# Delta recurrence: products that share an operand joined (48 in place of 80 a step), in two chains half a step apart, with keys and queries interleaved by chunk

## The chip, the cores and the metric

The kernel runs on one core of one Trainium2 chip. The metric is the device time of one execution in microseconds (us). A run gives one time; the figure quoted for a kernel is the median of its runs.

## The reference, cut to what matters

Four model layers follow one another over `x`, 16 sequences of 512 tokens with 128 channels. The change lies in the mixing part of layer 1, a gated delta rule with 4 heads of 32 channels, in chunks of 32 tokens (16 chunks a sequence):

```python
def _delta_rule(q, k, v, beta):
    ...
    v = v * beta[..., None]
    kb = k * beta[..., None]
    ...
    A = jnp.where(tril_strict, kb @ jnp.swapaxes(k, -1, -2), 0.0)
    inv = solve_triangular(eye + A, jnp.broadcast_to(eye, A.shape), lower=True)
    u = inv @ v
    w = inv @ kb
    ...
    def step(S, xs):
        q_i, k_i, u_i, w_i = xs
        attn = jnp.where(tril, q_i @ jnp.swapaxes(k_i, -1, -2), 0.0)
        u_adj = u_i - w_i @ S
        o_i = q_i @ S + attn @ u_adj
        S = S + jnp.swapaxes(k_i, -1, -2) @ u_adj
        return (S, o_i)
    S, o = jax.lax.scan(step, S0, (qs, ks, us, ws))
```

Both kernels compute `u_adj` as `inv @ (v - kb @ S)`, so that `inv` is applied once. The state `S` of a head is 32x32 and runs through the 16 chunks one after the other; 16 sequences by 4 heads are independent.

## The kernel before, in words

The program is written engine by engine: each engine (PE, DVE, ACT, POOL, and SP for the DMAs) has its own list of instructions in a fixed order, and semaphores tie them together. There is no scheduler; the order written is the order run. `l1_attn` (L1085 on) runs five phases with a barrier of all engines between them: `delta_inputs`, `delta_inverse`, `delta_recurrence`, `long_convolutions`, `delta_output`. The first three hand their tensors on through DRAM (`k.d`, one 128x512 array a sequence and name).

`delta_inputs` (L1104 on) handles one sequence a round: projections, filters, norms, and at the end on DVE `scale` (L1183 on) and `mask_products` (L1199 on), which write the tensors that the recurrence reads: `k` (tokens of a chunk by channels), `qT` and `kbT` (channels by tokens), `vb`, `a` and `attnT`. Every one is 128x512: row block h (32 rows) is head h, column block n (32 columns) is chunk n. SP stores 8 tensors a round (L1306). `delta_inverse` makes `inverseT` from `a`.

`delta_recurrence` (L1393 on) takes 4 sequences (G) at a time, a group; 4 groups run after one another, the first unrolled, the other three in a hardware loop (`over_groups`). A group has 16 steps, one a chunk. In a step all 4 sequences by 4 heads go through the same products, 16 products of 32x32 by 32x32 each, on the diagonal tiles of the array (rows and columns of head h): `tiles`, L1454. In the order of PE (`run` in the PE block):

- `ps_r` = kb S; DVE (L1512) makes `r` = vb - ps_r;
- `ps_u` = inv r; ACT (L1546) copies it to `u`;
- `ps_s` = kᵀ u; DVE (L1516) adds it to the state, which goes back and forth between two buffers;
- `ps_o` = q S + attn u of the step before, 32 products, in two halves put into the places where PE waits for `r` and for `u`; ACT (L1538) copies it out.

That is 80 products a step. In the loop a small `carrier` product (L1461) stands ahead of each wait. Every 4 steps, a quarter, DVE transposes the quarter's output (L1526), SP stores it and loads the same quarter of the next group: 6 loads of 128 partitions by 4 sequences by 128 columns (L1428), one store (L1434). All four quarters of a group are loaded before the first starts.

## Time and profile before

| what | value |
|---|---|
| median of 3 runs | 5998.68 us (5989.8 to 6001.67) |
| the profiled execution: its time | 5983.12 us |
| the profiled execution: its span | 5981.3 us |
| busy over the span: PE / weight loads / DVE / ACT / POOL | 75% / 47% / 67% / 39% / 30% |
| mean granted TensorE clock | 0.833 of full speed |

The span is the time from the first to the last instruction of the profiled execution. Busy shares are means over twelve stages with different limits; the change touches two phases of one stage. Rows name lines of the kernel before (L1454), engines (PE matmul, PEld weight load, DVE VectorE, ACT ScalarE, SPq the DMA issues of SyncE) and tiles by the program's names without buffer numbers; most tiles of the recurrence lie in a spare tensor and so are shown as `convolved`. "issue" as the reason of a wait means that the engine waited for nothing that the profile shows. An f32 matmul is shown as two weight loads and two matmuls, so 16 products are 32 matmul rows.

### The profile page before, as it was taken

Reading aid. Unit: us, or ns where it says so; the run is one execution under the profiler, and the core shown is the slowest. Engines: PE = TensorE matmul, PEld = TensorE weight load, DVE = VectorE, ACT = ScalarE, POOL = GpSimd, SP = SyncE. Lnnn points to the kernel's source line nnn. Section 1 sums busy time; section 2 is a strip of 40 time slices with the busy share of each in tenths; the row PEclk is TensorE's granted clock in tenths of the full one; section 3 lists DMA queues with packets and bytes.
Section 4 is the critical chain, followed back from the end, with each engine's and each line's share of the span. In section 5 each row is a group of like instructions: output and inputs, shape, how many; then the busy total and the mean of one; then the engine's idle time right before and its main releaser. Section 6 shows DMA issues by size and latency. Waiting matters only on the chain. (4 is left out here: it accounts for less than half of the span.)

```text
span 5981.3 us, 117856 instructions
## 1 busy us (share of the span) xinstructions
PE 4490.3 (75%) x44057; PEld 2811.6 (47%) x44057; DVE 4032.7 (67%) x9213; ACT 2353.0 (39%) x4425; POOL 1785.9 (30%) x2265
## 2 busy tenths in 40 slices
PE   4699998596720665674966669999666799888998
PEld 3122222484410554453744434544344577666776
DVE  6688885787977112786879757777698455485553
ACT  3488887202410103442111146666311344323443
POOL 2455552212433000233124334443244111163110
PEclk9699999798865557765987769999877899888999
DMA  1222220001331425100000023222000000000001
GB/s 41 50 51 51 51 51 19 6 1 49 117 94 38 114 77 104 52 32 21 1 1 0 3 51 63 58 53 52 1 0 0 20 0 0 1 1 1 0 0 29
DMA packets 229468, 203.06 MB, mean 34 GB/s; under 512 B 24067, under 2 KB 202879, under 8 KB 228399
## 3 DMA queue, kind: packets, MB, share of 16 engines
q1 hardware_dynamic: 229039, 197.19, 14.2%
q8 instruction: 288, 4.72, 0.3%
q14 instruction: 141, 1.16, 0.1%
HBM read 118.89 MB, written 72.88 MB: 32 GB/s over the span
## 5 line engine op out<-in xcount | busy, mean ns | idle before, releaser
L534 DVE TENSOR_REDUCE rotary_maxima<-rotary_ps_s 128x1 f32<-128x512 f32 x1024 | 644.3, 684 | 120.1 <-PE rotary_ps_s L697 118.2
L534 DVE TENSOR_REDUCE alibi_maxima<-alibi_ps_s 128x1 f32<-128x128 f32 (+3 forms) x1024 | 451.8, 485 | 233.0 <-PE alibi_ps_s L705 226.3
L782 ACT ACTIVATE rotary_probs<-rotary_ps_s 128x512 f32<-128x512 f32 x1024 | 552.5, 596 | 130.6 <-PE rotary_ps_s L721 128.1
L2161 DVE SCALAR_TENSOR_TENSOR x<-moe_ps_out,moe_weights,x 128x128 f32 (+1 forms) x1024 | 285.6, 344 | 458.2 <-PE moe_ps_out L2202 430.5
L2202 PEld LDWEIGHTS moe_ps_out<-w_moe_w,moe_hidden 128*128 128x128 f32 x4096 | 495.0, 192 | 108.2 <-issue 80.4
L2202 PE MATMUL moe_ps_out<-w_moe_w,moe_hidden 128*128 128x128 f32 x4096 | 500.6, 275 | 0.0
L2189 PE MATMUL moe_ps_hidden<-moe_z,w_moe_w 128*128 128x512 f32 x1024 | 488.7, 600 | 0.0
L2251 ACT ACTIVATE moe_hidden<-moe_ps_hidden,w_moe_b 128x512 f32<-128x512 f32 x512 | 345.6, 687 | 360.2 <-PE moe_ps_hidden L2189 348.4
L782 ACT ACTIVATE alibi_probs<-alibi_ps_s 128x512 f32<-128x512 f32 (+3 forms) x1024 | 394.4, 440 | 214.4 <-PE alibi_ps_s L729 211.3
L697 PE MATMUL rotary_ps_s<-rotary_k_stack,rotary_q_stack 64*128 64x512 bf16 x1024 | 251.2, 404 | 49.6 <-DMA rotary_k_stack<-rotary_parts 25.0
L217 POOL TENSOR_TENSOR moe_rstd<-moe_meanvar,eps 128x4 f32<-128x4 f32 x64 | 12.8, 201 | 907.7 <-DVE moe_meanvar L190 907.7
L662 PE MATMUL rotary_ps_pv<-rotary_probs,rotary_v 128*32 128x512 f32 x2048 | 277.4, 614 | 2.8 <-ACT rotary_probs L782 1.2
L1025 PE MATMUL moe_ps_out<-w_moe_w,moe_weighed 128*128 128x128 f32 x2048 | 270.2, 287 | 1.9 <-DVE moe_weighed L960 1.9
L1025 PEld LDWEIGHTS moe_ps_out<-w_moe_w,moe_weighed 128*128 128x128 f32 x2048 | 246.7, 197 | 39.2 <-issue 33.1
L2054 PE MATMUL fp_ps_gate<-w_fp_gate,fp_normedT 128*128 128x352 f32 x256 | 141.3, 643 | 149.7 <-DVE fp_hidden L2015 127.7
L697 PE MATMUL alibi_ps_s<-alibi_k_stack,alibi_q_stack 64*128 64x128 bf16 (+3 forms) x1024 | 209.0, 316 | 54.1 <-DMA alibi_k_stack<-alibi_parts 28.4
L697 PEld LDWEIGHTS rotary_ps_s<-rotary_k_stack,rotary_q_stack 64*128 64x128 bf16 x1024 | 64.7, 93 | 385.9 <-DVE rotary_maxima L534 291.8
L721 PE MATMUL rotary_ps_s<-rotary_q_stack,rotary_k_stack 64*128 64x512 bf16 x1024 | 220.8, 382 | 21.3 <-ACT rotary_probs L782 12.5
L2189 PEld LDWEIGHTS moe_ps_hidden<-moe_z,w_moe_w 128*128 128x128 f32 x1024 | 175.7, 192 | 128.2 <-issue 123.9
L1454 PE MATMUL delta_state_ps_r<-convolved 32*32 32x32 f32 x2048 | 44.6, 239 | 251.5 <-DMA convolved<-delta_attnT 237.3
L1546 ACT COPY convolved<-delta_state_ps_u 128x128 f32<-128x128 f32 x64 | 17.0, 266 | 493.6 <-PE delta_state_ps_u L1454 493.6
L960 DVE TENSOR_TENSOR moe_weighed<-moe_normedT,moe_ps_spread 128x1024 f32<-128x1024 f32 x128 | 152.6, 1211 | 81.9 <-PE moe_ps_spread L1016 81.9
(488 smaller groups left out, 10715.2 us busy)
## 6 DMA issues: line engine op xcount, KB each, us to landing
rotary_parts<-rotary_part SPq DMA_DIRECT2D x96, 128.0 KB, 2.2
rotary_q_stack<-rotary_parts SPq DMA_DIRECT2D x192, 64.0 KB
rotary_k_stack<-rotary_parts SPq DMA_DIRECT2D x192, 64.0 KB
convolve_bands<-in_filters SPq DMA_DIRECT2D x192, 64.0 KB, 2.6
alibi_parts<-alibi_part SPq DMA_DIRECT2D x96, 128.0 KB, 2.4
alibi_q_stack<-alibi_parts SPq DMA_DIRECT2D x192, 64.0 KB
alibi_k_stack<-alibi_parts SPq DMA_DIRECT2D x192, 64.0 KB
delta_n<-convolved SPq DMA_DIRECT2D x16, 256.0 KB, 2.0
```

The costliest lines, as they stand in the source:

```text
L534: v.tensor_reduce(maxima[:, blk, 2 * pair + two:2 * pair + two + 1], ps_s1[(j - 1 + u) % 3][:, 0:keys_of(blk)], AXIS.X, ALU.max).then_inc( ...
L662: last = mm(ps_pv[32 * g:32 * g + 32, lo:T], va[jv][:, kb, 4 * qd + g, :], probs[4 * (group % 2) + g][:, 0:T - lo], start=(kb == 0), stop= ...
L697: last = mm(ps_s1[(jb + u) % 3][:, 0:n], qs[jb][rows, pair, blk * P:(blk + 1) * P], ks[jb][rows, pair, 0:n], start=True, stop=not causal)
L721: last = mm(ps_s2[(jc + u) % 3][:, 0:T - lo], ks[jc][rows, pair, kb * P:(kb + 1) * P], qs[jc][rows, pair, lo:T], start=True, stop=not causal)
L782: nc.scalar.activation(probs[u % 8][:, 0:T - lo], ps_s2[(j - 2 + u) % 3][:, 0:T - lo], ACT.Exp).then_inc(s.exp_made, 1)
L960: v.tensor_tensor(weighed[n][:], nT, ps_spread[n % 2][:], ALU.mult).then_inc(s.inputs_weighed, 1)
L1025: last = mm(ps_out[i % 2][:, b, :], weighed[n][:, m, b * P:(b + 1) * P], w.moe1_w[:, 2 * n + m, :], start=(n + m + b == 0), stop=False)
L2054: nc.tensor.matmul(ps_gate[b % 2][:], nT[:, b * P:(b + 1) * P], w.fp4_gate[:, 0:F], start=True, stop=True).then_inc(s.gate_done, 1)
L2161: v.scalar_tensor_tensor(xb, ps_out[e % 2][:, b:b + 1, :], weights[par][:, b, e:e + 1], xb, ALU.mult, ALU.add).then_inc(s.added, 1)
L2189: mm(ps_hidden[(2 * e + h) % RING][:], w.moe3_w1[:, e, h * P:(h + 1) * P], z[par][:], start=True, stop=True).then_inc(s.hidden_done, 1)
L2202: last = mm(ps_out[e % 2][:, b, :], hidden[e % 2][:, h, b * P:(b + 1) * P], w.moe3_w2[:, e, h, :], start=(h == 0), stop=(h == 1))
L2251: nc.scalar.activation(hidden[e % 2][:, h, :], ps_hidden[(2 * e + h) % RING][:], ACT.Gelu, bias=w.moe3_b1[:, e, h:h + 1]).then_inc(s.hidde ...
```

## The change

`delta_inputs` writes two wide tensors in place of four: `kq`, in which for each chunk the 32 columns of `kbT` and the 32 of `qT` stand side by side, and `ku`, the same for `k` and `attnT`. SP stores 6 tensors a round. The arithmetic is the same; DVE writes `k`, `attnT`, `qT` and `kbT` with a stride of 64 columns a chunk.

`delta_recurrence` has three blocks of 16 products a step: `first` (`kq` against the state: kb S and q S at once, 64 output rows), `make_u` (inv r), `third` (`ku` against u: the step of the state and attn u at once, 64 output rows). The operands of `first` and of `make_u` lie on the partitions 0 to 31 (heads 0 and 1) and 64 to 95 (heads 2 and 3); heads 0 and 1 differ by a column offset. `make_r`, the sum of the state and the new sum of the output (`o1` + attn u) on DVE, and the copy `keep_o1` on ACT, go over 128x256. Two chains of 4 sequences run half a step apart; two turns of 16 double steps handle the 16 sequences; nothing is in a hardware loop. Each chain has two buffers a quarter of input: 13 loads a quarter and chain (12 of 32 partitions, one of 128), 4 stores.

```diff
-                 for n in ("a", "inverseT", "kbT", "qT", "k", "vb", "attnT", "n", "v", "o")}
+                 for n in ("a", "inverseT", "kq", "ku", "vb", "n", "v", "o")}
...
+    kq, ku = [[ph.sb(f"{n}{j}", [P, CHUNKS, 2, CHUNK]) for j in range(2)] for n in ("kq", "ku")]
...
-                k_out, qT_out, kbT_out = [out[n][par] for n in ("k", "qT", "kbT")]
+                k_out, qT_out, kbT_out = ku[par][:, :, 0, :], kq[par][:, :, 1, :], kq[par][:, :, 0, :]
...
-                v.transpose(qT_out[:], qn[:]).then_inc(s.back_turned, 1)
+                v.transpose(qT_out, by_chunk(qn)).then_inc(s.back_turned, 1)
...
+    rows = lambda h: slice(h * DH, (h + 1) * DH)
+    low = lambda h: slice(h // 2 * 2 * DH, (h // 2 * 2 + 1) * DH)
+    pair = lambda h: slice(h // 2 * 2 * DH, (h // 2 + 1) * 2 * DH)
...
+            def load(g, c, q):
+                j = q % RING
+                for h in range(GH):
+                    for to, name in ((kq, "kq"), (vb, "vb"), (inverseT, "inverseT")):
+                        sp.dma_start(flat(to[c][j][low(h), h % 2]), seq_rows(name, g, c, q)[rows(h)]).then_inc(loaded[c][j], 16)
+                sp.dma_start(flat(ku[c][j][:]), seq_rows("ku", g, c, q)).then_inc(loaded[c][j], 16)
...
+                        sp.wait_ge(o_turned[c], Q * g + q + 1)
+                        if q + RING < Q:
+                            load(g, c, q + RING)
+                        elif g + 1 < turns:
+                            load(g + 1, c, q + RING - Q)
+                        for h in range(GH):
+                            sp.dma_start(seq_rows("o", g, c, q)[rows(h)], o_cm[c][q % RING][h // 2 * 2 * DH + DH:h // 2 * 2 * DH + 2 * DH, h % 2]).then_inc(stored[c][q % RING], 16)
...
+            def first(g, c, i):
...
+                pe.wait_ge(state_made[c], n + g + 1)
+                at_least(pe, o1_kept[c], n)
+                for b in range(G):
+                    for h in range(GH):
+                        last = mm(ps_first[c][pair(h), h % 2, b, :], kq[c][q % RING][low(h), h % 2, b, i % Q, :],
+                                  state[c][i % 2][low(h), h % 2, b, :], start=True, stop=True)
...
+            def make_u(g, c, i):
...
+                        last = mm(ps_u[c][rows(h), b, :], inverseT[c][q % RING][low(h), h % 2, b, i % Q, :], r[c][low(h), h % 2, b, :],
+                                  start=True, stop=True)
...
+            def third(g, c, i):
...
+                        last = mm(ps_third[c][pair(h), h % 2, b * DH:(b + 1) * DH], ku[c][q % RING][rows(h), b, i % Q, :],
+                                  u[c][rows(h), b, :], start=True, stop=True)
...
                 for i in range(CHUNKS):
+                    first(g, 0, i)
+                    if i:
+                        third(g, 1, i - 1)
+                    make_u(g, 0, i)
+                    first(g, 1, i)
+                    third(g, 0, i)
+                    make_u(g, 1, i)
+                third(g, 1, CHUNKS - 1)
...
+                v.tensor_tensor(r[c][:], vb[c][q % RING][:, :, :, i % Q, :], ps_first[c][:], ALU.subtract).then_inc(r_made[c], 1)
...
+                v.tensor_tensor(state[c][(i + 1) % 2][:], state[c][i % 2][:], thirds[c], ALU.add).then_inc(state_made[c], 1)
...
+                v.tensor_tensor(o_hc[c][i // Q % 2][:, :, :, i % Q, :], o1[c][:], thirds[c], ALU.add).then_inc(o_added[c], 1)
...
                 for i in range(CHUNKS):
+                    make_r(g, 0, i)
+                    if i:
+                        add(g, 1, i - 1)
                     if i and i % Q == 0:
+                        turn(g, 1, i // Q - 1)
+                    make_r(g, 1, i)
+                    add(g, 0, i)
+                    if i % Q == Q - 1:
+                        turn(g, 0, i // Q)
...
+                    keep_o1(g, 0, i)
+                    keep_u(g, 0, i)
+                    keep_o1(g, 1, i)
+                    keep_u(g, 1, i)
```

On PE, in the recurrence, one step of the kernel before (the second of a group: r, half of o, u, the other half of o, s, and the next r) reads:

```order
L1454 MATMUL delta_state_ps_r<-convolved 32x32 x16
L1454 MATMUL delta_state_ps_o0<-convolved 32x32 x16
L1454 MATMUL delta_state_ps_u<-convolved 32x32 x16
L1454 MATMUL delta_state_ps_o0<-convolved 32x32 x16
L1454 MATMUL delta_state_ps_s<-convolved 32x32 x16
```

In the changed kernel one double step, a step of each chain (the number after `first`, `u` and `third` is the chain), reads on PE:

```order
L1475 MATMUL delta_state_ps_first0<-convolved 64x32 x16
L1495 MATMUL delta_state_ps_third1<-convolved 64x32 x16
L1484 MATMUL delta_state_ps_u0<-convolved 32x32 x16
L1475 MATMUL delta_state_ps_first1<-convolved 64x32 x16
L1495 MATMUL delta_state_ps_third0<-convolved 64x32 x16
L1484 MATMUL delta_state_ps_u1<-convolved 32x32 x16
```

A step of 5 blocks of 16 has become 3 blocks of 16, and behind each block of one chain stands a block of the other; `third1` belongs to the step before.

On SP, one load of a quarter for 4 sequences in the kernel before, six issues:

```order
L1428 DMA convolved<-delta_kbT 128x4x128
L1428 DMA convolved<-delta_vb 128x4x128
L1428 DMA convolved<-delta_inverseT 128x4x128
L1428 DMA convolved<-delta_k 128x4x128
L1428 DMA convolved<-delta_qT 128x4x128
L1428 DMA convolved<-delta_attnT 128x4x128
```

In the changed kernel the same quarter of one chain begins with the three rows of head 0, which follow three times more for heads 1 to 3, and ends with `ku`; the stores of an earlier quarter come behind it:

```order
L1442 DMA convolved<-delta_kq 32x4x256
L1442 DMA convolved<-delta_vb 32x4x128
L1442 DMA convolved<-delta_inverseT 32x4x128
...
L1443 DMA convolved<-delta_ku 128x4x256
L1456 DMA delta_o<-delta_state_o_cm00 32x4x128 x4
```

Six loads and a store have become 13 loads and 4 stores, with the same bytes; the store, which stood ahead of the loads, stands behind them.

## Rows read from the trace of the kernel before

**Rows 1.** Busy time by stretch: `delta_inputs`, then the recurrence's lead-in, steps, end.
```profile
core 0: us, PE busy (x) PEld busy (x) DVE busy (x) ACT busy (x) POOL busy (x), PEclk, DMA share, GB/s
1385.00:1725.00 340.00, 206.99 (x4533) 121.40 (x4531) 275.92 (x583) 130.11 (x192) 115.75 (x64) 0.80 0.29 105
1937.00:1944.50 7.50, 0.00 (x0) 0.00 (x0) 0.17 (x1) 0.00 (x0) 0.00 (x0) 0.50 0.82 229
1944.50:2271.20 326.70, 221.21 (x10432) 186.60 (x10432) 48.71 (x147) 34.09 (x128) 0.00 (x0) 0.50 0.33 88
2271.20:2275.70 4.50, 0.00 (x0) 0.00 (x0) 0.00 (x0) 0.00 (x0) 0.00 (x0) 0.50 0.19 58
```

**Rows 2.** Waits of PE, 1944 to 2275: us in total, times, longest us.
```profile
PE delta_state_ps_o L1454 <- issue: 32.2, 34, 3.1
...
PE delta_state_ps_s L1454 <- issue: 14.8, 14, 1.3
PE delta_state_ps_u L1454 <- issue: 11.4, 13, 2.3
PE delta_state_ps_r L1454 <- issue: 7.8, 11, 1.5
PE delta_state_ps_carrier L1461 <- issue: 7.2, 2, 3.7
```

**Rows 3.** DMA queues, 1945 to 2271: packets, MB, share of 16 engines.
```profile
q1 hardware_dynamic: 54870, 27.24, 30.6%
q8 instruction: 84, 1.38, 1.8%
```

**Rows 4.** Timeline of PE, 2127 to 2136: start, us, instruction, [idle before <- releaser].
```profile
2127.50 0.65 PE L1454 MATMUL delta_state_ps_r<-convolved 32*32 32x32 f32 x31 [0.15 <-issue]
...
2129.33 0.63 PE L1454 MATMUL delta_state_ps_o<-convolved 32*32 32x32 f32 x30
2131.39 0.26 PE L1454 MATMUL delta_state_ps_o<-convolved 32*32 32x32 f32 x2 [1.43 <-issue]
...
2135.39 0.28 PE L1454 MATMUL delta_state_ps_u<-convolved 32*32 32x32 f32 x4 [0.55 <-issue]
```

**Rows 5.** DMA queues, 1950 to 2024, the first group, with the loads of the second.
```profile
q1 hardware_dynamic: 17099, 8.49, 43.0%
q8 instruction: 19, 0.31, 1.7%
```

**Rows 6.** DMA queues, 2189 to 2271, the last group, which loads nothing further.
```profile
q1 hardware_dynamic: 5280, 2.62, 11.6%
q8 instruction: 23, 0.38, 1.8%
```

**Rows 7.** Groups by line and shape, 1944.5 to 2271.2: busy us, mean ns, idle before.
```profile
L1454 PE MATMUL delta_state_ps_r<-convolved 32*32 32x32 f32 x2048 | 44.6, 239 | 251.5 <-DMA convolved<-delta_attnT 237.3 <-issue 7.8 <-DVE convolved L1516 6.4
...
L1516 DVE TENSOR_TENSOR convolved<-convolved,delta_state_ps_s 128x128 f32<-128x128 f32 x64 | 18.4, 288 | 208.0 <-PE delta_state_ps_s L1454 208.0
L1512 DVE TENSOR_TENSOR convolved<-convolved,delta_state_ps_r 128x128 f32<-128x128 f32 x64 | 18.4, 288 | 70.1 <-PE delta_state_ps_r L1454 68.7
...
L1546 ACT COPY convolved<-delta_state_ps_u 128x128 f32<-128x128 f32 x64 | 17.0, 266 | 493.6 <-PE delta_state_ps_u L1454 493.6
L1526 DVE STREAM_TRANSPOSE convolved<-convolved 128x512 f32<-128x512 f32 x16 | 11.4, 711 | 6.8 <-ACT convolved L1538 6.3
```

**Rows 8.** Groups by line and shape, whole run: a wider DVE operation and one transpose.
```profile
L862 DVE TENSOR_TENSOR moe_more<-moe_more,moe_same 128x256 f32<-128x256 f32 x32 | 13.6, 425 | 1.1
...
L1193 DVE STREAM_TRANSPOSE convolved<-convolved 128x512 f32<-128x512 f32 x16 | 11.3, 705 | 0.0
```

**Rows 9.** Timeline of SP, 1936 to 2140: DMA issues, the first loads and later ones.
```profile
1937.26 0.40 SPq L1428 DMA_DIRECT2D convolved<-delta_kbT  x1
1937.71 0.50 SPq L1428 DMA_DIRECT2D convolved<-delta_vb  x1
...
1939.91 0.71 SPq L1428 DMA_DIRECT2D convolved<-delta_attnT  x1
...
1945.75 0.83 SPq L1428 DMA_DIRECT2D convolved<-delta_kbT  x1
```

**Rows 10.** Timeline of PE, 2340 to 2343, `long_convolutions`: 64-column tiles over all rows.
```profile
2340.32 0.94 PE L1614 MATMUL convolve_ps_y<-convolve_windows,convolve_bands 128*64 128x64 f32 x24 [0.80 <-DMA convolve_bands<-in_filters]
```

**Rows 11.** Busy time by stretch: loads of `a` in `delta_inverse`, 16 partitions each, 8 apart.
```profile
1726.00:1740.00 14.00, 0.00 (x0) 0.00 (x0) 0.97 (x1) 0.00 (x0) 9.00 (x1) 0.50 1.13 193
```

More of the change, by code:

```diff
@@ L1407, in delta_recurrence @@
-    state = [ph.sb(f"state{j}", [P, G, DH]) for j in range(2)]
-    o_hc = [ph.sb(f"o_hc{j}", [P, G, Q, DH]) for j in range(2)]
-    o_cm = [ph.sb(f"o_cm{j}", [P, G, Q * DH]) for j in range(Q)]
-    ps_r, ps_u, ps_s = ph.ps("r", [P, G, DH]), ph.ps("u", [P, G, DH]), ph.ps("s", [P, G, DH])
-    ps_o = [ph.ps(f"o{j}", [P, G, DH]) for j in range(2)]
-    ps_carrier = ph.ps("carrier", [DH, 1])
-    groups = seqs // G
-    seq_rows = lambda name, g, q: d[name][bass.ds(g * G, G), :, q * (T // Q):(q + 1) * (T // Q)].rearrange("s p t -> p s t")
@@ L1416, in over_groups @@
-    def over_groups(eng, run):
-        run(0)
-        if groups > 1:
-            with eng.Fori(1, groups) as g:
-                run(g)
+    CHAINS = 2
+    RING = 2
+    LOADS = 3 * GH + 1
+    per_chain = "first_done r_made o1_kept u_done u_made third_done state_made o_added o_turned".split()
+    s = [ph.signals(" ".join([f"{n}{c}" for n in per_chain] + [f"loaded{c}_{j} stored{c}_{j}" for j in range(RING)])) for c in range(CHAINS)]
+    first_done, r_made, o1_kept, u_done, u_made, third_done, state_made, o_added, o_turned = [
+        [s[c][n] for c in range(CHAINS)] for n in range(len(per_chain))]
@@ new lines, in delta_recurrence @@
+    r, o1 = [[ph.sb(f"{n}{c}", [P, 2, G, DH]) for c in range(CHAINS)] for n in ("r", "o1")]
+    u = [ph.sb(f"u{c}", [P, G, DH]) for c in range(CHAINS)]
+    state = [[ph.sb(f"state{c}{j}", [P, 2, G, DH]) for j in range(2)] for c in range(CHAINS)]
+    o_hc = [[ph.sb(f"o_hc{c}{j}", [P, 2, G, Q, DH]) for j in range(2)] for c in range(CHAINS)]
+    o_cm = [[ph.sb(f"o_cm{c}{j}", [P, 2, G, Q * DH]) for j in range(RING)] for c in range(CHAINS)]
+    ps_first = [ph.ps(f"first{c}", [P, 2, G, DH]) for c in range(CHAINS)]
@@ new lines, in delta_recurrence, with seq_rows @@
+    ps_u = [ph.ps(f"u{c}", [P, G, DH]) for c in range(CHAINS)]
+    ps_third = [ph.ps(f"third{c}", [P, 2, T]) for c in range(CHAINS)]
+    thirds = [ps_third[c][:, :, 0:G * DH].rearrange("p e (b v) -> p e b v", v=DH) for c in range(CHAINS)]
+    turns = seqs // (G * CHAINS)
+    rows = lambda h: slice(h * DH, (h + 1) * DH)
+    low = lambda h: slice(h // 2 * 2 * DH, (h // 2 * 2 + 1) * DH)
+    pair = lambda h: slice(h // 2 * 2 * DH, (h // 2 + 1) * 2 * DH)
+    def seq_rows(name, g, c, q):
+        wide = d[name].shape[2] // Q
+        first = (CHAINS * g + c) * G
+        return d[name][first:first + G, :, q * wide:(q + 1) * wide].rearrange("s p t -> p s t")
@@ L1422, in delta_recurrence @@
+    flat = lambda t: t.rearrange("p b n e -> p b (n e)")
     with nc.Block() as block:
@@ L1448, in _ @@
             mm = nc.tensor.matmul
-            def tiles(to, left, right, start=True, stop=True, sequences=range(G)):
-                for b in sequences:
-                    for h in range(GH):
-                        at = slice(h * DH, h * DH + DH)
-                        last = mm(to[at, b, :], left[at, b, :], right[at, b, :], start=start, stop=stop)
-                return last
-            def ready(sem, value):
-                at_least(pe, sem, value)
-                if not isinstance(value, int):
-                    mm(ps_carrier[0:DH, 0:1], k.ident16[:, 0:DH], k.ident16[:, 0:1], start=True, stop=True)
@@ L1463, in results @@
-            def results(g, i, sequences):
-                if 0 in sequences:
-                    ready(s.o_read, CHUNKS * g + i - 1)
-                q, c = i // Q, slice((i % Q) * CHUNK, (i % Q + 1) * CHUNK)
-                for b in sequences:
-                    tiles(ps_o[i % 2], t["qT"][:, q, :, c], state[i % 2], stop=False, sequences=[b])
-                    last = tiles(ps_o[i % 2], t["attnT"][:, q, :, c], u[i % 2], start=False, sequences=[b])
-                if G - 1 in sequences:
-                    last.then_inc(s.o_done, 1)
@@ L1522, in turn, with make_r @@
-            def turn(g, q):
-                dve.wait_ge(s.o_read, CHUNKS * g + Q * q + Q)
-                at_least(dve, stored[q], 16 * g)
-                v.transpose(o_cm[q][:].rearrange("p b t -> p (b t)"),
-                            o_hc[q % 2][:].rearrange("p b n e -> p (b n e)")).then_inc(s.o_turned, 1)
-            over_groups(dve, run)
+            def make_r(g, c, i):
+                n, q = CHUNKS * g + i, i // Q
+                dve.wait_ge(first_done[c], n + 1)
+                if i % Q == 0:
+                    dve.wait_ge(loaded[c][q % RING], here(g, q))
+                at_least(dve, u_done[c], n)
+                v.tensor_tensor(r[c][:], vb[c][q % RING][:, :, :, i % Q, :], ps_first[c][:], ALU.subtract).then_inc(r_made[c], 1)
```

164 lines of the change are left out of this document (77 added, 87 removed).

## The prediction

> **What bounds the kernel now.** I began with the busy time by stretch [rows 1]. The recurrence has three stretches: a lead-in of 7.5 us with no product, 326.7 us of steps, and an end of 4.5 us, together 338.7 us. In the steps DVE is busy for 48.7 us and ACT for 34.1 us, PE for 221 us, and the DMA engines for a third. No engine is full, so the waits come next. Among PE's waits [rows 2] five rows name "issue": 32.2 + 14.8 + 11.4 + 7.8 + 7.2 = 73.4 us in 74 pieces. PE then waited for nothing that a semaphore shows. The DMA queues [rows 3] show 84 packets of instructions, 1.38 MB, so 16.4 KB each, in this stretch; PE has 2 x 10432 loads and matmuls in it, 248 a packet. The timeline [rows 4] shows a stall at 2127.50, one of 1.43 us before 2131.39 and one of 0.55 us before 2135.39: 3.9 and 4.0 us apart, with 31 + 1 + 32 + 1 + 32 + 30 = 127 matmuls between the first two (of which some rows are left out), thus 254 records. So PE stops at each packet's end until the next has come, about 0.87 us each time (73.4 / 84). A packet every 3.89 us (326.7 / 84) is what PE lives on. With 43% of the DMA engines taken, 19 packets came in 74 us, 3.89 us each [rows 5]; with 11.6% taken, 23 in 82 us, 3.57 us each [rows 6]. This is the reader's main point: time goes with the **number of PE instructions**. The granted clock is 0.50 throughout [rows 1], the 1.2 GHz level; a rise would change nothing in a sum paced by packets.
>
> The other part of a step is the chain through the engines: r on DVE 288 ns, the state on DVE 288 ns, u on ACT 266 ns, three blocks of matmuls [rows 7], each 0.65 us for 16 products [rows 4].
>
> **The change, part by part.**
>
> *Fewer products.* Before there are 64 steps of 4 sequences with 80 products each, 5120 (with 192 carriers 10432 matmuls, two a product). Now there are 32 double steps of 2 x 4 sequences with 96 products each, 3072: 6144 matmuls, 12288 records, and at 248 a packet 49.5 packets.
>
> *What a double step takes without stalls.* One chain's round: `first` takes 0.82 + 0.24 us, as heads 0 and 1 use the same tiles of the array and I let its products start at half the pace of the 0.65 us block (0.41 us for its starts, 0.24 for the last one); make_r 0.425 us, for 128x256 on DVE [rows 8]; make_u 0.65; keep_u 0.27; third 0.65; the state 0.425. Sum 3.48 us. The other chain's block often stands ahead on PE, whose starts alone take 2 x (0.82 + 0.41 + 0.41) = 3.28 us. DVE has 6 x 0.425 and half a transpose of 1024 columns (2 x 0.705 [rows 8], each chain every fourth step: 0.7 us a double step), 3.25 us. I take 4.5 us, between 3.48 (perfect overlap) and twice that, 6.96 (none).
>
> *What the packets make of it.* A double step has 384 records, 1.55 packets. At 4.0 us a packet that is 6.2 us, above 4.5, so **the instructions' supply covers the longer DVE operations, `keep_o1`, the second chain's order on PE and the lost carriers**; if that cover is gone, 4.5 us are left (rival A). Read the other way, as 0.87 us of stall added to the work, it is 4.5 + 1.55 x 0.87 = 5.85 us, nearly the same. I take 4.0 us a packet rather than 3.89, since the same bytes come in less time: 27.24 MB [rows 3] at 30.6% of 326.7 us are 50% of 200 us, more than the 43% of the first group. 49.5 x 4.0 = **198 us**. Ends: 3.57 us, the quiet group, gives 177; 4.5 us, twice as far above the quiet group as the loaded one is and a little more, 223.
>
> *Lead-in.* Before, six issues and 3.6 us to the last landing. Now the first chain waits for 13 issues. Those early ones come 0.45 to 0.53 us apart (1937.26, 1937.71, the sixth at 1939.91) [rows 9]: 6.5 + 3.6 = **10 us**, instead of 7.5. Ends: 9 and 17 us (13 x 0.85, the later spacing, + 3.6 + some 2 for the other chain's).
>
> *End.* 4.5 us now; three more stores at 0.4 us, half a transpose more 0.7, and eight more semaphores to clear, for which no row stands: between nothing and an issue's 0.4 us each I take 0.6 us in all, nearer to nothing, as all 18 of before lie within the 4.5 us. That makes **7 us**, between 6 and 10.
>
> *SP's queue.* Seventeen issues for each chain and quarter, 16 of these. Later issues take 0.83 us [rows 9], so 14.5 us for one group and 231 us in all at that spacing; at 0.45 us 122. They run beside the steps, 4 double steps of 6.2 us = 25 us for two such groups. At 0.45 us (15 us) they are hidden, at 0.83 us (29 us) they aren't: rival C. Nothing else waits on SP; a load stands behind the wait for `o_turned`, the stores behind the loads, so `o_cm` comes free later by 11 issues, which a ring of two quarters covers.
>
> *`delta_inputs`.* DVE is its bound, 276 of 340 us [rows 1]. Six stores rather than eight then cost and give nothing. The strided writes: the nearest rows are `make_r` before, which reads `vb` with a stride between blocks of 32 columns, and the state's add, which does not: both 288 ns [rows 7]. Hence I take 0. Upper end: three transposes of 0.705 us doubled in 16 rounds, 34 us; lower end 0, as no operation is shortened.
>
> *Sum.* 198 + 10 + 7 = 215 us for 338.7, a gain of 123 us. The profiled execution took 5983.1 us, 15.6 below the median of the three runs, 5998.7; 5998.7 - 123 = **5876 us**. By the ends of the packets (177 and 223) 5855 and 5901, with the other terms' ends about 5850 to 5910.
>
> **The rivals.**
>
> *A, the supply isn't what binds.* If the stalls come from something that the changed order doesn't meet, a double step takes 4.5 us: 32 x 4.5 + 17 = 161, a gain of 178, 5821 us. Against it: 74 stalls in 84 packets, in every group [rows 2, 3]. The Trainium skill (Runtime: NRT & Kernel Launch, "Instruction fetch mechanics") says that the engine's memory is refilled in blocks of 16 KiB, 256 instructions, while the current one runs, and that this is hidden by the rate of issue. The size agrees with the 16.4 KB and 248 of these rows; that it is hidden does not. Chance 0.10.
>
> *B, the shared rows make PE slow.* Heads 0 and 1 of `first` and `make_u` load their weights from the same 32 rows. If each such load waits for the matmul ahead of it, `first` starts a matmul every 60 ns, not 26, and make_u every 30: I take the 30 from the 24 matmuls of the convolution, which all share their rows, (0.94 - 0.24) / 23 us [rows 10], and double it for two heads on one tile. PE then has 2 x (1.92 + 0.97 + 0.41) = 6.6 us a double step, 8.0 with stalls; at the middle, 7.3, 234 + 17 = 251 us, a gain of 88: 5911 us. Rows 10 alone, at 30 ns for both, would stay under the packets' 6.2 us, which speaks against B. The Trainium skill (TensorE: Matmul & The Clock Gate, "Part 3: Packing small matmuls") speaks for B: a weight load overlaps a running matmul only where the row group differs, and the change brings four row groups down to two. Chance 0.10.
>
> *C, SP's queue binds.* At 0.83 us an issue the 16 groups take 231 us; with the lead-in and end 248, a gain of 91, 5908 us. For it: the spacing while the first loads are in flight [rows 9]; against it: the average of DMA activity, which stays near half. Chance 0.12.
>
> *E, the chains don't overlap.* Then 6.96 us and 1.35 of stalls, 32 x 8.3 + 17 = 283 us: 5943 us. Against it: the order on PE puts a block of the other chain behind each block. Chance 0.05.
>
> *D, slower.* 12 of 13 loads, and all stores, touch 32 neighbouring partitions. If such a transfer gets a quarter of the rate, 229 GB/s in the lead-in of before [rows 1], thus 57, then a chain's quarter (1.05 MB so, 0.52 MB in `ku`, 0.26 MB out) takes 18.3 + 2.3 + 4.6 = 25 us, and 16 of them 403 us: with 17 us 82 more than before, 6081 us. It decides from (338.7 - 17) / 16 = 20 us a group on. Against it: loads of 16 partitions ran at 193 GB/s [rows 11]; but their partitions lie 8 apart, so this doesn't exclude D. Chance 0.08.
>
> **How the numbers follow.** 0.2% is 12 us, about what a measurement of this kernel can tell from no change. The forecast has 0.55, with 5850 to 5910 as its own range; A 0.10, B 0.10, C 0.12, E 0.05, all faster by far more than 12 us: 0.92. D's 0.08 reaches from break-even up; I give 0.01 of it to no change and 0.07 to slower. The range 5820 to 5925 holds the forecast, B, C and the upper half of A; left out are D, E, the rest of A, and a tail of the forecast, 0.2.
>
> **What would show it.** Right: about 50 packets of instructions between the first and the last product, stalls by "issue" every 127 matmuls or so, double steps near 6.2 us, and the stage near 215 us; DVE at 425 ns, the clock at 0.50; `delta_inputs` still 340 us with the same transposes. C shows as PE's waits for `loaded` ahead of a quarter; B as a `first` far above 1.06 us; A as steps of 4.5 us without stalls; D as loads that land after more than 15 us. Wrong would be the forecast if PE waits mostly for DVE or ACT, for then the chain and not the supply sets the pace.

## The result, and the profile after

The changed kernel takes 5890.6 us (median of 4 runs, 5886.28 to 5895.65), the kernel before on the same chip 5994.24 us. The ratio is 0.9832, 95% interval 0.9819 to 0.9844. The forecast was 5876 us with a range of 5820 to 5925: sign and range held. The gain is 103.6 us where 123 were forecast. The profile shows that the number came out near for another reason than the one given.

The profiled execution took 5886.28 us. First the busy time by stretch: `delta_inputs`, then the recurrence's lead-in to the first product, the time from there to the second chain's first product, the steps, and the end.

```profile
core 0: us, PE busy (x) PEld busy (x) DVE busy (x) ACT busy (x) POOL busy (x), PEclk, DMA share, GB/s
1385.00:1725.00 340.00, 208.66 (x4538) 122.39 (x4537) 275.05 (x584) 129.92 (x192) 115.65 (x64) 0.80 0.28 105
1938.57:1947.93 9.36, 0.00 (x0) 0.00 (x0) 0.54 (x2) 0.00 (x0) 0.00 (x0) 0.50 0.69 193
1947.93:1955.01 7.08, 2.58 (x64) 2.32 (x64) 0.42 (x1) 0.64 (x2) 0.00 (x0) 0.50 1.14 239
1955.01:2169.80 214.79, 211.01 (x6072) 201.01 (x6076) 92.72 (x206) 40.14 (x126) 0.00 (x0) 0.50 0.45 122
2169.80:2178.35 8.55, 0.44 (x18) 0.30 (x12) 2.49 (x4) 0.00 (x0) 0.00 (x0) 0.50 0.26 62
```

The recurrence takes 9.36 + 7.08 + 214.79 + 8.55 = 239.8 us in place of 338.7. In the steps PE is busy for 211.0 of 214.8 us; before, it was busy for 221 of 327 [rows 1]. The waits of PE in the recurrence say the same (238.6 us of the first row are the phase ahead of it, in which PE has nothing to do; the other 4.0 are the second chain's wait for its loads):

```profile
PE delta_state_ps_first L1475 <- DMA convolved<-delta_ku: 242.6, 2, 238.6
PE delta_state_ps_first L1475 <- issue: 2.5, 1, 2.5
PE delta_state_ps_u L1484 <- DVE convolved L1519: 1.0, 2, 0.5
PE delta_state_ps_third L1495 <- ACT convolved L1568: 0.8, 2, 0.4
```

"issue" has gone from 73.4 us in 74 pieces [rows 2] to one piece of 2.5 us, and the waits for DVE and ACT are 1.8 us in all. The packets of instructions come as before; the DMA queues from 1955 to 2170:

```profile
q8 instruction: 48, 0.79, 1.6%
```

48 packets in 215 us are one in 4.48 us, slower than the 3.57 to 3.89 us of the kernel before [rows 5, 6]. So in the changed kernel it is PE that takes its time with a packet, and the next one is there when it is wanted. What PE does with the time is in its timeline, two half steps:

```profile
1957.73 0.65 PE L1484 MATMUL delta_state_ps_u<-convolved 32*32 32x32 f32 x32
1958.34 1.80 PE L1475 MATMUL delta_state_ps_first<-convolved 32*64 32x32 f32 x29
...
1959.98 1.14 PE L1495 MATMUL delta_state_ps_third<-convolved 32*64 32x32 f32 x30
1961.06 0.65 PE L1484 MATMUL delta_state_ps_u<-convolved 32*32 32x32 f32 x32
1961.66 1.80 PE L1475 MATMUL delta_state_ps_first<-convolved 32*64 32x32 f32 x29
```

A half step is 3.33 us (1957.73 to 1961.06), a double step 6.65, without a gap: 0.61 us until `first` starts, 1.64 until most of `third` starts, 1.08 until the next `u`. `first` has 29 of its matmuls in 1.80 us; less 0.29 us for the last one that is 1.51 / 28 = 54 ns from start to start. `third`, with the same shape, has (1.14 - 0.29) / 29 = 29 ns, `u` (0.65 - 0.24) / 31 = 13 ns. The groups by line and shape:

```profile
L1475 PE MATMUL delta_state_ps_first<-convolved 32*64 32x32 f32 x2048 | 123.9, 291 | 245.1 <-DMA convolved<-delta_ku 242.6 <-issue 2.5
...
L1495 PE MATMUL delta_state_ps_third<-convolved 32*64 32x32 f32 x2048 | 81.2, 290 | 0.8 <-ACT convolved L1568 0.8
...
L1484 PE MATMUL delta_state_ps_u<-convolved 32*32 32x32 f32 x2048 | 41.7, 239 | 1.0 <-DVE convolved L1519 1.0
...
L1519 DVE TENSOR_TENSOR convolved<-convolved,delta_state_ps_first 128x256 f32<-128x256 f32 x64 | 27.0, 422 | 109.1 <-PE delta_state_ps_first L1475 109.1
```

`first` alone holds PE for 123.9 us, more than half of the steps. Its heads 0 and 1 load weights of 64 columns into the same 32 rows and 64 columns of the array. `third` has the same weights' width, but its heads lie on rows of their own; `u` shares rows, but each head has columns of its own. Call the rows and columns of the array that a product uses its tile: `first` then works on two tiles, `third` and `u` on four.

### The profile page after: what moved, and what is told of

Same layout as the page of the kernel before. It is cut to its first block and busy times, and to the rows that moved or that the text cites. A ratio compares the mean times of both kernels' runs of the same rounds, so it can differ in the third digit from the quotient of the medians.

```text
span 5884.5 us, 109248 instructions
## 1 busy us (share of the span) xinstructions
PE 4476.3 (76%) x39769; PEld 2821.3 (48%) x39769; DVE 4080.4 (69%) x9277; ACT 2358.3 (40%) x4425; POOL 1782.7 (30%) x2265
## 5 line engine op out<-in xcount | busy, mean ns | idle before, releaser
L1475 PE MATMUL delta_state_ps_first<-convolved 32*64 32x32 f32 x2048 | 123.9, 291 | 245.1 <-DMA convolved<-delta_ku 242.6
L1475 PEld LDWEIGHTS delta_state_ps_first<-convolved 32*64 32x64 f32 x2048 | 115.7, 215 | 251.0 <-DMA convolved<-delta_ku 242.8
```

The costliest lines, as they stand in the source:

```text
L1475: last = mm(ps_first[c][pair(h), h % 2, b, :], kq[c][q % RING][low(h), h % 2, b, i % Q, :], state[c][i % 2][low(h), h % 2, b, :], start=Tr ...
```

## The experiments

The theory after the result has two parts. **Tiles**: `first` is slow because its products go to only two tiles of 32 rows by 64 columns, one for two heads, where they follow one another; that weight load and matmul take turns there, as the expectations below have it, is an assumption that no run tests. **Supply**: packets of instructions come at a limited pace, and bind where PE would be faster than that, as before the change. Rivals are the order of the heads in PE's queue, shared rows as such, a cost added at each packet's end, and the chain through DVE and ACT. In the table the recurrence runs from its first load to the first load of the next phase (338.5 before, by this measure); `delta_inputs` from its first to its last instruction; "issue" is the sum of PE's stalls by issue in the recurrence.

| kernel | time, us | recurrence | `delta_inputs` | issue |
|---|---|---|---|---|
| before | 5994.24 | 338.5 | 314.3 | 73.4 |
| changed | 5890.6 | 239.8 | 315.2 | 2.5 |
| heads_order | 5875.09 (one run) | 242.9 | 310.7 | 3.3 |
| split_first | 5912.87 (one run) | 287.1 | 313.6 | 74.8 |
| rows4 | 5906.23 | 225.3 | 342.5 | 33.9 |
| apart | 5949.43 (one run) | 304.0 | 313.9 | 2.5 |
| rows4b | 5871.52 | 231.6 | 319.2 | 38.3 |
| no_o | 5901.9 (one run) | 257.3 | 313.7 | 17.4 |
| no_loads | 5868.16 (one run) | 209.5 | 319.7 | 16.0 |
| rows4c | 5868.38 | 218.4 | 320.6 | 23.5 |
| changed_again | 5893.39 | 242.3 | 309.5 | 3.5 |
| rows4c_again | 5868.83 | 217.0 | 319.0 | 23.9 |

Single times differ by some 15 us with nothing changed in the stage (heads_order against the changed kernel), and the kernels ran on several chips, so the stage is what the single runs are read by.

**heads_order.**

```diff
-                    for h in range(GH):
+                    for h in (0, 2, 1, 3):
                         last = mm(ps_first[c][pair(h), h % 2, b, :], kq[c][q % RING][low(h), h % 2, b, i % Q, :],
```

> The heads of `first` are taken in the order 0, 2, 1, 3, all else as changed. Theory 1 (tiles): heads 0 and 1 share one tile of 32 rows by 64 columns, heads 2 and 3 another, and on a tile weight load and matmul take turns, 107 ns a matmul; both tiles already run side by side, so the order does not matter: `first` stays at 1.7 us for its starts, a half step at 3.33 us, the recurrence at 240 us (within 3). Rival (order): PE takes its queue in order and a product behind one on the same tile holds up the rest; alternating tiles then lets `first` fall to the pace of `third`, 33 ns a matmul, 1.07 us: 64 x 0.64 = 41 us less, 199 us.

Measured: no gain, 242.9 us, as the changed kernel itself had in a later run (242.3, below). The timeline of its PE has the same spacing, 3.33 us from `u` to `u`:

```profile
2053.82 0.65 PE L1484 MATMUL delta_state_ps_u<-convolved 32*32 32x32 f32 x32
2054.45 1.80 PE L1475 MATMUL delta_state_ps_first<-convolved 32*64 32x32 f32 x29
...
2057.15 0.65 PE L1484 MATMUL delta_state_ps_u<-convolved 32*32 32x32 f32 x32
```

The order of the heads does not matter; the rival falls.

**split_first.**

```diff
-                    for h in range(GH):
-                        last = mm(ps_first[c][pair(h), h % 2, b, :], kq[c][q % RING][low(h), h % 2, b, i % Q, :],
+                    for a in range(2):
+                        for h in range(GH):
+                            last = mm(ps_first[c][rows(h // 2 * 2 + a), h % 2, b, :], kq[c][q % RING][low(h), h % 2, b, i % Q, a * CHUNK:(a + 1) * CHUNK],
```

> `first` is split again into two products of 32 columns a head, kb S and q S, on the same 32 rows but on column tiles of their own (128 products a double step in place of 96). Theory 1 (tiles) alone: such products run like make_u, 19 ns a matmul, so `first` takes 64 x 0.019 = 1.2 us in place of 1.7 and a half step 2.9 us in place of 3.33: 27 us less than 240. Theory 2 (instruction supply, the forecast's): 512 records a double step are 2.06 packets at 3.57 to 4.0 us, 7.4 to 8.3 us in place of 6.65: 23 to 52 us more, with PE's stalls by issue back. If weight loads on shared rows never overlap (the skill's rule, rival B), `first` gets no shorter and the double step is at least 6.65 us.

Measured: 287.1 us, 47 more, inside the supply's 23 to 52. Its PE timeline and the waits:

```profile
2052.07 0.65 PE L1485 MATMUL delta_state_ps_u<-convolved 32*32 32x32 f32 x32
2052.65 1.15 PE L1476 MATMUL delta_state_ps_first<-convolved 32*32 32x32 f32 x64
2053.74 1.06 PE L1496 MATMUL delta_state_ps_third<-convolved 32*64 32x32 f32 x29
2055.76 0.42 PE L1496 MATMUL delta_state_ps_third<-convolved 32*64 32x32 f32 x3 [0.97 <-issue]
```

```profile
PE delta_state_ps_u L1485 <- issue: 35.0, 25, 3.9
PE delta_state_ps_third L1496 <- issue: 33.4, 31, 3.0
PE delta_state_ps_first L1476 <- issue: 6.4, 6, 2.5
```

Both parts show at once. The same arithmetic in twice as many products of half the width takes 1.15 us in place of 1.8: (1.15 - 0.24) / 63 = 14 ns a matmul. Heads 0 and 1 are on the same 32 rows as before, and they still share each tile; but kb S and q S now have columns of their own, so four tiles of 32 by 32 are at work where `first` had two of 32 by 64. So neither shared rows nor a tile shared by two heads is slow as such; how many tiles are at work, and how wide they are, is left. `ps_first` lies in PSUM as in the changed kernel, so its place there is not the cost either. And PE, which is then faster, waits for its instructions again: 74.8 us of issue. Joining products pays here because it takes fewer instructions, not because PE's array is quicker.

**rows4.**

```diff
+                            for a in range(2):
+                                sp.dma_start(far[at, :, 1 - a, :], t[par][at, :, a, :]).then_inc(stored[par], 16)
...
-                for h in range(GH):
-                    for to, name in ((kq, "kq"), (vb, "vb"), (inverseT, "inverseT")):
-                        sp.dma_start(flat(to[c][j][low(h), h % 2]), seq_rows(name, g, c, q)[rows(h)]).then_inc(loaded[c][j], 16)
+                for to, name in ((kq, "kq"), (vb, "vb"), (inverseT, "inverseT"), (ku, "ku")):
+                    sp.dma_start(flat(to[c][j][:]), seq_rows(name, g, c, q)).then_inc(loaded[c][j], 16)
...
-                        last = mm(ps_first[c][pair(h), h % 2, b, :], kq[c][q % RING][low(h), h % 2, b, i % Q, :],
-                                  state[c][i % 2][low(h), h % 2, b, :], start=True, stop=True)
+                        last = mm(ps_first[c][pair(h), h % 2, b, :], kq[c][q % RING][rows(h), b, i % Q, :],
+                                  state[c][i % 2][rows(h), h % 2, b, :], start=True, stop=True)
```

The two planes of `ps_first` lie in banks of their own, which the chains share; `first` waits for both chains' `o1`.

> For heads 1 and 3 the halves of kq and ku are swapped (by the stores of delta_inputs, 16 a sequence in place of 6), so that kb S and the state of head h lie on rows of head h: `first` and make_u use four groups of 32 rows, and a quarter of a chain needs 4 loads of 128 partitions in place of 13; 96 products a double step as before. Theory 1 (tiles): `first` falls to the pace of `third`, 33 ns a matmul, a half step to 1.07 + 1.07 + 0.61 = 2.75 us: a double step of 5.5 us. Theory 2 (supply): 384 records are 1.55 packets at 3.57 to 4.0 us: 5.5 to 6.2 us, with stalls by issue back where PE would be faster. With 5 to 8 us less of lead-in the recurrence takes 196 to 220 us in place of 240 under both, nearer 200 without theory 2. Theory 3 (the chain through DVE and ACT sets 6.65 us): steps unchanged, only the lead-in shorter, 233 us. Unknown: what stores with pieces of 128 bytes add to delta_inputs; between 0 and 4 us a sequence.

Measured: recurrence 225.3 us, but `delta_inputs` 342.5, the whole 5906.23 us, 15.6 above the changed kernel's median, though on another chip and with intervals of the ratio that overlap (0.9856, 0.9831 to 0.9882). In the recurrence, a few rows of the timeline of PE and its waits:

```profile
2056.57 1.06 PE L1483 MATMUL delta_state_ps_first<-convolved 32*64 32x32 f32 x29
2059.80 0.31 PE L1483 MATMUL delta_state_ps_first<-convolved 32*64 32x32 f32 x2 [2.16 <-issue]
...
2061.59 1.08 PE L1483 MATMUL delta_state_ps_first<-convolved 32*64 32x32 f32 x32
```

```profile
PE delta_state_ps_third L1503 <- issue: 15.0, 9, 3.1
PE delta_state_ps_first L1483 <- issue: 13.7, 9, 3.4
PE delta_state_ps_u L1492 <- issue: 5.2, 10, 1.2
```

`first`, the same 32 matmuls with the same 64 columns, takes 1.08 us in place of 1.92 (which is what it takes in "apart" below, where it stands alone): (1.08 - 0.29) / 31 = 25 ns. Four tiles of 64 columns are at work now. rows4 also moves the planes of `ps_first` to other banks, but split_first lost the slow starts without that. Together: with four tiles at work matmuls start 13 to 14 ns apart where the weights have 32 columns and 25 to 29 ns apart where they have 64; with two tiles of 64 columns, 54 ns. Half the tiles doubles the spacing, and so does twice the width. A spacing times the tiles at work gives, as an estimate, some 55 ns for a matmul on a tile of 32 columns and some 105 on one of 64; what a tile does in that time, no run shows.

And again, as PE gets faster, its stalls by issue return, 33.9 us. The time, 225.3 us, is outside the 196 to 220 that both parts of the theory gave. From the first product to the last it is 210 us: some 175 of work, as theory 1 had it (32 x 5.5 = 176), and the 33.9 of stalls, more than the 22 by which 6.2 us a double step would exceed that. The chain's theory (233 us) falls by the waits rather than by the time: PE waits 1.8 us in all for DVE and ACT. The price stands in `delta_inputs`, among the waits of ACT there:

```profile
ACT convolved L1277 <- DMA delta_ku<-convolved: 67.3, 14, 5.5
```

**apart.**

```diff
-                    first(g, 0, i)
-                    if i:
-                        third(g, 1, i - 1)
-                    make_u(g, 0, i)
-                    first(g, 1, i)
-                    third(g, 0, i)
-                    make_u(g, 1, i)
-                third(g, 1, CHUNKS - 1)
+                    for c in range(CHAINS):
+                        first(g, c, i)
+                        make_u(g, c, i)
+                        third(g, c, i)
```

DVE's order follows in the same way.

> The two chains run one after the other in each double step (first, make_u, third of chain 0, then of chain 1), same products, loads and widths. Theory 1 (tiles; PE is full when the chains interleave): the waits for r and for u come out: 1.8 + 0.5 + 0.65 + 0.35 + 1.14 = 4.45 us a chain, 8.9 a double step, so 32 x 2.25 = 72 us more than 240. Theory 2 (supply sets the pace): hidden up to 6.2 us, the rest shows: between 0 and 70 us more. If the half-step offset does nothing, no change.

Measured: 304.0 us, 64 more; 72 were expected. The waits of PE that have come out, and one chain's part of a step:

```profile
PE delta_state_ps_u L1484 <- DVE convolved L1515: 36.4, 64, 0.7
PE delta_state_ps_third L1495 <- ACT convolved L1558: 24.6, 64, 0.4
```

```profile
2051.86 1.92 PE L1475 MATMUL delta_state_ps_first<-convolved 32*64 32x32 f32 x32
2054.30 0.65 PE L1484 MATMUL delta_state_ps_u<-convolved 32*32 32x32 f32 x32 [0.52 <-DVE convolved L1515]
2055.33 1.07 PE L1495 MATMUL delta_state_ps_third<-convolved 32*64 32x32 f32 x32 [0.39 <-ACT convolved L1558]
```

The half step's offset hides the two waits, 61 us; it is worth about as much as all of that.

**no_o**, made from the kernel before.

```diff
-                    tiles(ps_o[i % 2], t["qT"][:, q, :, c], state[i % 2], stop=False, sequences=[b])
-                    last = tiles(ps_o[i % 2], t["attnT"][:, q, :, c], u[i % 2], start=False, sequences=[b])
+                    if b == G - 1:
+                        last = tiles(ps_o[i % 2], t["attnT"][:, q, :, c], u[i % 2], sequences=[b])
```

> The kernel before, with 52 products a step in place of 80: of the output's 32 products only four are left (attn u of the last sequence), which ACT copies to all four places; the output of layer 1's mixing is left out so. It asks how the packets bound the kernel before. By pace (a packet every 3.57 to 3.9 us, work beside it): 214 records a step are 0.86 packets, 3.1 to 3.4 us, the chain of r, u and state 3.3 us: about 3.4 us a step, 218 us of steps in place of 327. By addition (each packet's end costs 0.87 us on top of the work, as the forecast's other reading has it): 3.3 + 0.86 x 0.87 = 4.05 us, 259 us. If neither instructions nor packets matter and the chain alone set 5.1 us a step: no change.

Measured: 257.3 us, less lead-in and end of 12 us 245 in the steps, 3.83 us a step. Neither number came out: pace had 218, addition 259. The waits tell why:

```profile
PE delta_state_ps_carrier L1461 <- DVE convolved L1516: 18.2, 45, 0.4
PE delta_state_ps_carrier L1461 <- DVE convolved L1512: 14.8, 48, 0.6
...
PE delta_state_ps_carrier L1461 <- issue: 7.7, 2, 3.9
```

With all of their rows, DVE and ACT hold PE for 66 us, issue for 17.4. The chain alone sets some 3.6 us a step, (245 - 17) / 64, not the 3.3 estimated; the DMA queues show 55 packets in 235 us, 4.27 us each, so most are there in time. Addition would have asked for 0.87 us at each of the 55, 48 us; 17.4 were seen. So the packets are a pace, not a toll, and the kernel before, at 5.1 us a step and 3.89 us a packet, was held by it, 73.4 us of it.

The packets' own times in the trace show this directly. In the steps of the kernel before, each of the 74 stalls by issue ends 1.2 to 1.8 us after a packet of 16 KB of the queue q8 has landed (median 1.4), though the stretches from 1.1 to 1.8 us behind a landing are only 18% of the time; of the 62 stalls of split_first 61 end in such a stretch too. The next packet starts 1.0 us or more after the stall's end (median 1.2) and takes 0.9 to 1.5 us (median 1.05), and no two overlap. So one packet comes after the other, and a round is some 3.6 us, by adding the medians: where PE needs longer than that for a packet's instructions, it need not stall. Beside loads, in the first group of before, the next packet starts up to 2.8 us after the stall's end, in the quiet last group up to 1.7, while a packet itself takes the same 0.9 to 1.4 us in both.

**rows4b.**

```diff
-                    sp.dma_start(d[n][bass.ds(i, 1)].rearrange("o p t -> (o p) t"), t).then_inc(stored[par], 16)
+                    sp.dma_start(d[n][bass.ds(i, 1)].rearrange("o p t -> (o p) t"), t).then_inc(early[par], 16)
...
                 dve.wait_ge(s.rs_made, i + 1)
+                before(dve, i, par, stored, 12)
```

> As rows4, but in delta_inputs ACT and the first DVE operations wait only for the four stores whose buffers they write again (a semaphore of their own); the twelve stores of kq and ku are waited for a stage later, in scale. Theory: the 27 us that rows4 lost in delta_inputs (342 in place of 315 us) came from ACT's 67 us of waits for a delta_ku store, not from the transfers themselves; then delta_inputs is back at 315 to 320 us, the recurrence stays at 223, and the whole is 12 to 17 us under the changed kernel (5890.6): 5874 to 5879 us. Rival: the small pieces load the DMA engines, and delta_inputs stays above 335 us, the whole at 5900.

Measured: `delta_inputs` 319.2 us, and the wait of ACT for a `delta_ku` store is gone, so that wait was the cause; 5871.52 us, ratio 0.9812 (0.9795 to 0.983) of the kernel before. The recurrence did not stay at 223 us: it took 231.6, with 38.3 us of issue. The row of the DMA engines' busy share, in tenths, 40 slices from 1950 to 2155, and two stretches with many loads, each with a quiet one behind it:

```profile
DMA  9200597003991019920049900079500598002200
```

```profile
1971.00:1982.30 11.30, 8.35 (x313) 7.62 (x311) 5.35 (x12) 1.95 (x7) 0.00 (x0) 0.50 0.89 274
1982.30:1997.90 15.60, 12.86 (x460) 11.68 (x460) 6.66 (x15) 3.17 (x10) 0.00 (x0) 0.50 0.15 43
1997.90:2009.40 11.50, 7.75 (x287) 7.05 (x280) 4.78 (x11) 1.92 (x6) 0.00 (x0) 0.50 0.83 252
2009.40:2024.90 15.50, 14.32 (x528) 13.34 (x525) 7.05 (x17) 3.19 (x10) 0.00 (x0) 0.50 0.19 57
```

With the DMA engines at 0.83 to 0.89, PE starts 600 matmuls in 22.8 us, 26 a us; at 0.15 to 0.19, 988 in 31.1, 32 a us. Four large loads a quarter come in a burst. That the packets wait in it is what the next two runs test.

**no_loads**, rows4b without the loads behind the first two quarters; the waits for them are adapted.

```diff
-                        if q + RING < Q:
-                            load(g, c, q + RING)
-                        elif g + 1 < turns:
-                            load(g + 1, c, q + RING - Q)
```

> rows4b with the loads of all quarters behind the first two left out (the first two quarters' data are used again; the recurrence's data are left out so). Theory (packets are slowed by load traffic): packets come every 3.57 us, as in the quiet group of before, and the steps take 49.5 x 3.57 = 177 us in place of 206. Rival (traffic does not matter, packets have one pace of 4.0 to 4.2 us): 200 to 208 us. PE's own work is 64 x 2.5 = 160 us: below that only if the supply does not bind at all.

Measured: 209.5 us, 22 less than rows4b, with 16.0 us of issue in place of 38.3. From the first product to the last it is 193 us: more than the theory's 177, less than the rival's 200. From 1960 to 2140 46 packets came, 3.91 us each, not the 3.57 expected, with PE still stalling a little at most of them:

```profile
PE delta_state_ps_first L1482 <- issue: 7.3, 13, 2.5
PE delta_state_ps_third L1502 <- issue: 4.7, 12, 1.3
PE delta_state_ps_u L1491 <- issue: 4.0, 10, 1.0
```

Traffic is thus 22 us of rows4b's recurrence, all of it in the stalls. The quiet pace is nearer to 3.9 us; why it was 3.57 in the last group of before stays open.

**rows4c.**

```diff
+                parts = [slice(0, G)] if g == 0 and q < RING else [slice(b, b + 1) for b in range(G)]
                 for to, name in ((kq, "kq"), (vb, "vb"), (inverseT, "inverseT"), (ku, "ku")):
-                    sp.dma_start(flat(to[c][j][:]), seq_rows(name, g, c, q)).then_inc(loaded[c][j], 16)
+                    for b in parts:
+                        sp.dma_start(flat(to[c][j][:])[:, b, :], seq_rows(name, g, c, q)[:, b, :]).then_inc(loaded[c][j], 16)
```

> As rows4b, but every load behind the first two quarters is split by sequence, 16 loads a chain and quarter in place of 4, which SP issues some 0.45 us apart: the same bytes over 7 us and more in place of a burst. Theory (packets of instructions wait in the bursts: in rows4b the packets take 5 to 7 us where the DMA engines are full, 3.4 to 4.0 elsewhere): the spread traffic lets PE stall less, the recurrence falls from 229 towards the 207 us without loads, to 212 to 222; the whole 5855 to 5865. Rival (what counts is the bytes, not their burst; or each DMA costs the queue the same): 229 within 4 us, the whole 5871 as rows4b.

Measured: recurrence 218.4 us, 13 less, the whole 5868.38 us, ratio 0.9797 (0.9772 to 0.9822). The DMA engines' row, 1950 to 2145, is level, and the stalls are 23.5 us:

```profile
DMA  0005564555645544565365505553555554520022
```

```profile
PE delta_state_ps_first L1488 <- issue: 10.1, 14, 2.5
PE delta_state_ps_third L1508 <- issue: 7.3, 13, 1.5
PE delta_state_ps_u L1497 <- issue: 6.1, 10, 0.9
```

The stage did what was expected of it; the whole fell less than the stage, 3 us by the medians, within the spread of these runs, and stayed above the 5855 to 5865 us expected.

**changed_again and rows4c_again**, the two kernels on one chip.

> The changed kernel once more, beside rows4c on one chip, so that the two are compared by the same runs of the kernel before. Expected: 0.983 of the kernel before (0.9819 to 0.9844 so far), recurrence 240 us with next to no stall by issue.

> rows4c beside the changed kernel on one chip. By the stages (recurrence 216 in place of 240 us, delta_inputs 320 in place of 315) it should be 19 us under the changed kernel, ratio 0.980; if the gain was the chip's or the run's, the two come out within 6 us of each other.

Measured: 5893.39 us, ratio 0.9842 (0.9825 to 0.9859), against 5868.83 us, ratio 0.9807 (0.979 to 0.9823). The intervals do not touch: rows4c is 24.6 us faster than the changed kernel, and the best of these kernels. Its recurrence is 25 us shorter, and `delta_inputs` 4 to 11 us longer for the swapped stores.

## Why the prediction was right, and where it was not

*What bounds the kernel before: right.* PE was held by the pace of its instructions. split_first brings 74.8 us of issue back by more instructions alone, no_o, with fewer, leaves 17.4, and every one of the 74 stalls of before ends 1.2 to 1.8 us after a packet has landed. The other reading, 0.87 us of stall added at each packet, falls: the changed kernel has 48 packets in its steps and 2.5 us of issue.

*49.5 packets at 4.0 us, 198 us: the step that failed.* The steps took 214.8 us, and the packets did not set them; of the prediction's own signs, stalls every 127 matmuls or so did not come. What was wrong is the work of a double step, 4.5 us in the prediction, 6.65 us in the trace. In it `first` was sized at 0.82 us for its starts by a guess (half the pace of the old block); that allowed for two tiles in place of four but not for weights twice as wide, and it takes 1.64 us until most of `third` starts. `third` was sized at 0.41 by the old block, though its weights are twice as wide; it is 1.08. `make_u` is 0.61 with the change-over. Twice 3.33 is above the 5.5 to 6.0 us that 1.55 packets need, and so the supply had slack for the first time. That the forecast came out near is luck: 6.65 and 6.2 lie close together, right in size, wrong in mechanism.

*Rival B is what happened, with its sign and half of its reason.* It had `first` at 60 ns a matmul (54 measured) and PE at 6.6 us a double step (6.65). That the two sums agree is luck in part: `first` was 1.92 (1.64 measured) and `make_u` 0.97 (0.61), too long, and `third` 0.41 (1.08), too short. Its time, 5911 us, was too long because it put stalls on top; a pace has none where PE is slower. Half of its reason holds: 30 ns for weights of 64 columns [rows 10], doubled for two heads on one tile, is near what was measured, 25 to 29 ns on four tiles and 54 on two. The other half, that weight loads on shared rows wait, is not what the runs show: `make_u` and split_first share rows, split_first its tiles too, and they run at 13 and 14 ns, as close as the block of before on four row groups ((0.65 - 0.24) / 31 = 13 ns). The Trainium skill (TensorE: Matmul & The Clock Gate, "Part 3: Packing small matmuls"), which has the row group decide, is not borne out by `make_u` and split_first; by `first` against rows4 it is. The number of tiles at work, with their width, fits all of them.

*Lead-in: 10 us, measured 9.36; but the second chain was left out.* It waits for 13 more loads: 7.08 us in which PE has 2.6 us of work. The upper end of the term held this, the sum did not. *End: 7 us, measured 8.55* with a part of the last `third`.

*`delta_inputs` at nothing: right.* Of the transposes, the one that writes `qT` with the stride (L1195) and the one that reads `k` with it (L1194) take as long as the same rows did before, 670 ns and the 705 of [rows 8]:

```profile
L1194 DVE STREAM_TRANSPOSE convolved<-convolved 128x512 f32<-128x512 f32 x16 | 11.3, 705 | 0.0
...
L1195 DVE STREAM_TRANSPOSE convolved<-convolved 128x512 f32<-128x512 f32 x16 | 10.7, 670 | 0.0
```

*Covers.* The 128x256 operations of DVE (422 ns, 425 forecast) and `keep_o1` (372 ns) are hidden, as said, but by PE's own work and not by the packets. *C and D fell*: SP issues 0.47 us apart, no product of a later quarter waits for a load, and 239 GB/s were moved in the stretch after the first product, when 12 of 13 loads were of 32 partitions. *E fell*: PE is full; "apart" shows that the offset is worth 64 us. *A* is half right: the stalls went, but not because fetching is hidden as such. The granted clock stayed at 0.50.

In sum: 215 us forecast for the stage, 239.8 measured: 16.8 more in the steps, 7.1 for the second chain, 1.6 at the end, 0.6 less in the lead-in. Behind the stage the convolution took 135.4 us in place of 132.0, in both profiles of the changed kernel, and 135.0 to 135.3 in heads_order, split_first and apart, but 131.7 to 132.8 in the kernels with the layout of rows4; why stays open. Between the two profiled executions of before and after the gain is 96.8 us, where the recurrence alone gives 98.7; the 103.6 of the medians is not accounted for in full.

*Slips in the working.* C's 14.5 and 231 us go by 0.85 us an issue; at the 0.83 that it names they are 14.1 and 226. The 4.5 us a packet of the upper end lies three times as far above the quiet 3.57 as the 3.89 measured beside loads, not twice. The stores are issued 13 to 16 places later than before, not 11. The sum of 215 us rests on none of them.

## What to carry to other kernels

Count an engine's instructions and compare their pace with the pace of the packets that bring them: where stalls by "issue" recur at a fixed count of instructions, fewer and wider instructions pay, and splitting them loses even when the engine itself would be faster. When such a limit is lifted, size the work beneath it from rows of the new shape before you trust it as cover: here wide weights on two tiles of the array took the limit's place. Large loads beside a kernel that lives on its instruction packets were better spread (218.4 us for the stage) than sent in a burst (231.6).

## What the runs showed of the hardware that was not expected

- The number of tiles at work and their width set the pace of small f32 matmuls, not the rows as such: on four tiles they start 13 to 14 ns apart with weights of 32 columns, even where two heads share rows (`make_u`) or tiles (split_first), 25 to 29 ns apart with 64 columns, and 54 ns apart on two tiles of 64 columns, all at the granted clock of 0.50.
- Instruction packets of 16 KB come one after the other: in the kernel before each of 74 stalls ends 1.2 to 1.8 us after one has landed, and the next starts 1.0 us or more after that.
- Instruction packets come later beside data: in rows4b PE starts 26 matmuls a us beside loads at 0.83 to 0.89 of the DMA engines, 32 beside 0.15 to 0.19; spreading the same bytes took 13 us off the stage, leaving the loads out 22.
- Sixteen stores a sequence in place of six, eight of them in pieces of 128 bytes, cost `delta_inputs` 4 to 11 us in 16 sequences once nothing waited for them, and 27 us while ACT did; the number of stores and the size of their pieces were not tried apart.
